# Opening and first turn of a fused attention kernel: GpSimd's and ScalarE's work reordered, q's first 128 pixels split apart, high blocks sent ahead of low ones

## The reference

```
q = Wq x + bq   (32 x 1024)      k = Wk x + bk   (32 x 1024)      v = Wv x + bv   (256 x 1024)
scores[i, j] = sum over channels of q[:, i] k[:, j]          (1024 x 1024)
attn = softmax(scores, over j)
out[:, i] = sum over j of v[:, j] attn[i, j]   + x[:, i]
```

## Time and profile before

| | us |
|---|---|
| median of three runs | 176.33 |
| the profiled execution's own time | 175.45 |
| its span | 173.3 |
| TensorE busy in it | 162.6 |
| VectorE busy | 137.0 |
| ScalarE busy | 110.6 |
| GpSimd busy | 41.1 |

### The profile page before, as it was taken

The page is one execution under the profiler, slowest core; times in us unless marked ns, Lnnn a source line. Parts: engine busy times, 40 slices in busy tenths (PEclk is TensorE's granted clock), DMA queues, the critical chain, the costliest instruction groups (busy, mean ns, idle before and its releaser), DMA issues.

```text
span 173.3 us, 2476 instructions
## 1 busy us (share of the span) xinstructions
PE 162.6 (94%) x814; PEld 129.9 (75%) x814; DVE 137.0 (79%) x215; ACT 110.6 (64%) x200; POOL 41.1 (24%) x50
## 2 busy tenths in 40 slices
PE   7979798978999999999999999999999999999992
PEld 5557676756888898767788898778888897776871
DVE  0779879888799898798899998799874889856353
ACT  2669594876985665777885665764884765665310
POOL 6249830042122030031222030042220020002500
PEclk9999999999999999999999999999999999999998
DMA  5941554034500320054400320054500330003003
GB/s 182 323 156 50 162 193 179 0 91 114 191 5 0 91 99 22 4 116 111 165 2 0 95 101 22 2 120 109 170 0 0 93 117 8 0 0 121 0 0 121
DMA packets 7500, 14.44 MB, mean 83 GB/s; under 512 B 1280, under 2 KB 1792, under 8 KB 7488
## 3 DMA queue, kind: packets, MB, share of 16 engines
q1 hardware_dynamic: 6656, 13.37, 24.0%
q0 software_dynamic: 416, 0.79, 2.1%
q10 hardware_dynamic: 416, 0.13, 0.3%
HBM read 4.59 MB, written 4.19 MB: 51 GB/s over the span
## 4 chain that ended last, share of the span: by engine, by line
PE 76%; DVE 12%; DMA 3%; ACT 3%; issue 2%; SPq 1%; DVEq 0%; ACTq 0%
PE acc L755 30%; PE acc L763 14%; PE slot L627 11%; PE st L741 8%; PE slot L680 7%; DVE negmax L514 5%; DMA wqk<-wqk_t 2%; DVE w_lo L557 1%; ACT dump L375 1%; SPq L195 1%; DMA k_a<-qk_parts 1%; PE slot L639 1%; PE st L726 1%; PE slot L644 1%; PE acc L759 1%
## 5 line engine op out<-in xcount | busy, mean ns | idle before, releaser
L755 PE MATMUL acc<-w_hi,v_hi 128*128 128x512 f32 x128 | 51.2, 400 | 0.0
L755 PE MATMUL acc<-w_hi,v_lo 128*128 128x512 f32 x128 | 50.5, 394 | 0.0
L406 ACT ACTIVATE w_full<-st 128x512 f32<-128x512 f32 x64 | 37.5, 594 | 17.1 <-PE st L741 17.1
L375 ACT ACTIVATE dump<-slot,negmax 128x1024 f32<-128x1024 f32 x29 | 32.4, 1117 | 13.5 <-DVE negmax L514 13.0
L314 POOL TENSOR_TENSOR w_lo<-w_full,w_hi 128x512 fp32r<-128x512 f32 x16 | 21.3, 1331 | 80.0 <-ACT w_full L406 64.0
L763 PE MATMUL acc<-w_lo,v_hi 128*128 128x512 f32 x120 | 38.4, 396 | 0.0
L514 DVE TENSOR_REDUCE negmax<-slot 128x1 f32<-128x1024 f32 x29 | 35.3, 1218 | 3.4 <-PE slot L680 3.4
L557 DVE TENSOR_TENSOR w_lo<-w_full,w_hi 128x512 fp32r<-128x512 f32 x48 | 33.2, 692 | 4.3 <-ACT w_full L406 0.6
L755 PEld LDWEIGHTS acc<-w_hi,v_hi 128*128 128x128 f32 x128 | 24.1, 189 | 5.6 <-issue 0.4
L548 DVE CAST w_hi<-w_full 128x512 fp32r<-128x512 f32 x47 | 19.9, 424 | 10.3 <-ACT w_full L406 9.1
L755 PEld LDWEIGHTS acc<-w_hi,v_lo 128*128 128x128 f32 x128 | 24.2, 189 | 5.2
(11 more groups left out here) (81 smaller groups left out, 178.5 us busy)
## 6 DMA issues: line engine op xcount, KB each, us to landing
out<-o_sb SPq DMA_DIRECT2D x7, 512.0 KB, 2.9
x_sb<-x SPq DMA_DIRECT2D x3, 1024.0 KB, 5.6
k_b<-k_a SPq DMA_DIRECT2D x8, 192.0 KB, 2.5
q_b<-q_a SPq DMA_DIRECT2D x8, 192.0 KB, 2.6
k_a<-qk_parts SPq DMA_DIRECT2D x12, 64.0 KB, 2.0
q_a<-qk_parts SPq DMA_DIRECT2D x12, 64.0 KB, 2.0
x_sb<-x SPq DMA_DIRECT2D x1, 512.0 KB, 3.6
x_sb<-x SPq DMA_DIRECT2D x2, 256.0 KB, 4.8
```

The source lines that it names most:

```text
L375: nc.scalar.activation(dump[:, t % 2, :], s_home(b, t), ACT.Exp, bias=negmax[:, t:t + 1], accum_out=rowsum[:, t:t + 1]).then_inc(rowsum_re ...
L406: nc.scalar.activation(w_full[:, r, :], st[:, j % 2, :], ACT.Exp).then_inc(exp_done, 1)
L755: nc.tensor.matmul(acc[:, c, :], v[:, j, ch], w_hi[:, r, :], start=(j == 0 and v is v_hi), stop=False)
```

## The change

- `cut_by_act` loses tile 7 of each turn: its `w_hi` is no longer a second exponential on ScalarE but a cast on VectorE.
- SP's `first_stacks` issues the high blocks of both halves, and then the low blocks of both, where it went half by half.
- `put_q_lo` takes a range of pixels, and runs for the first 128 pixels, the next 384, and the second half: three operations for two. The waits for `q_lo_put` are recounted, and `first_scores(1)` gets a wait for the second of them.
- `wv_hi` is made by GpSimd, which waits for the last `x_lo` of image 0 and for wv; it and `wv_lo` stand ahead of GpSimd's first `put_q_dup`, where `wv_lo` stood behind it.
- On ScalarE `sum_exp(0, TH)` goes from ahead of the first turn to behind its first exponential (tile 2), and `cut_x` in each step goes behind `put_rows`.

```diff
--- before.py
+++ after.py
@@ -32,7 +32,7 @@
 
 
     def cut_by_act(n):
-        return n % PER in ((0, 1, 7, 9, 11) if n < PER else (0, 7, 9, 11))
+        return n % PER in ((0, 1, 9, 11) if n < PER else (0, 9, 11))
 
 
     def split_by_pool(n):
@@ -230,6 +230,7 @@
                     sp.wait_ge(qk_cut_done, 2 * (b - 1) + h + 1)
                     blocks(sp, k_a, 0, 0, h, ka_in[h])
                     blocks(sp, q_a, 0, 1, h, qa_in[h])
+                for h in range(2):
                     sp.wait_ge(qk_split, 2 * (b - 1) + h + 1)
                     blocks(sp, k_a, 1, 2, h, ka_in[h])
                     blocks(sp, q_a, 2, 3, h, qa_in[h])
@@ -241,7 +242,7 @@
                 sp.wait_ge(k_lo_put, h + 1)
                 sp.wait_ge(k_hi_put, h + 1)
                 second_stack(k_b, k_a, h, kb_in[h])
-                sp.wait_ge(q_lo_put, h + 1)
+                sp.wait_ge(q_lo_put, h + 2)
                 sp.wait_ge(q_dup_put, h + 1)
                 second_stack(q_b, q_a, h, qb_in[h])
             for b in range(2, BATCH):
@@ -330,18 +331,22 @@
                     parts[:, :, :].bitcast(fp32).rearrange("p c (g d r) -> p c g d r", g=2, d=2)[:, :, :, 0, :],
                 ).then_inc(pair_made, 1)
             pool.wait_ge(pair_made, 2)
-            put_q_dup(0)
-            pool.wait_ge(q_dup_put, 1)
+
+            pool.wait_ge(x0_split, 4)
+            pool.wait_ge(wv_in, DMA)
+            nc.gpsimd.tensor_copy(wv_hi[:, :, :], wv[:, :, :]).then_inc(wv_cut, 1)
             pool.wait_ge(wv_cut, 1)
             nc.gpsimd.tensor_tensor(wv_lo[:, :, :], wv[:, :, :], wv_hi[:, :, :].bitcast(fp32),
                                     ALU.subtract).then_inc(wv_split, 1)
+            pool.wait_ge(wv_split, 1)
+            put_q_dup(0)
+            pool.wait_ge(q_dup_put, 1)
             prepare_x1(0)
             pool.wait_ge(x1_split, 1)
             put_q_dup(1)
             pool.wait_ge(q_dup_put, 2)
             for i in range(1, 3):
                 prepare_x1(i)
-
             pool.wait_ge(shift_ready, 1)
             prepare_x1(3)
             for n in range(TILES):
@@ -427,8 +432,6 @@
             put_k_hi(1)
             put_q_hi(0)
             put_q_hi(1)
-            act.wait_ge(wv_in, DMA)
-            nc.scalar.activation(wv_hi[:, :, :], wv[:, :, :], ACT.Copy).then_inc(wv_cut, 1)
             for t in range(TH):
                 sum_exp(0, t)
             log_sums(0, 0)
@@ -438,17 +441,18 @@
             exp(0)
             first_cut_v(3)
             exp(1)
-            sum_exp(0, TH)
 
             def turn(b):
                 for s in range(PER):
                     if PER * b + s + AHEAD < TILES:
                         exp(PER * b + s + AHEAD)
-                    if s in CUT_X and b + 2 < BATCH:
-                        cut_x(b + 2, CUT_X.index(s))
+                    if b == 0 and s == 0:
+                        sum_exp(0, TH)
                     what, k, image = front(b, s)
                     if what == ROW:
                         put_rows(b + image, k)
+                    if s in CUT_X and b + 2 < BATCH:
+                        cut_x(b + 2, CUT_X.index(s))
                     what, t, image = front(b, s - 1)
                     if what == S:
                         sum_exp(b + image, t)
@@ -490,12 +494,15 @@
                     out=k_a[2 * CQK:3 * CQK, cols(h)], in0=qk_home(0, h)[0:CQK, :], scalar=bias[0:CQK, 0:1],
                     in1=k_a[0:CQK, cols(h)].bitcast(fp32), op0=ALU.add, op1=ALU.subtract).then_inc(k_lo_put, 1)
 
-            def put_q_lo(h):
+            def put_q_lo(part):
+
+                h = part.start // HALF
                 rows = slice(2 * CQK, 3 * CQK)
                 dve.wait_ge(q_hi_put, h + 1)
                 nc.vector.scalar_tensor_tensor(
-                    out=q_a[CQK:2 * CQK, cols(h)], in0=qk_home(0, h)[rows, :], scalar=bias[rows, 0:1],
-                    in1=q_a[rows, cols(h)].bitcast(fp32), op0=ALU.add, op1=ALU.subtract).then_inc(q_lo_put, 1)
+                    out=q_a[CQK:2 * CQK, part], in0=qk_home(0, h)[rows, part.start - h * HALF:part.stop - h * HALF],
+                    scalar=bias[rows, 0:1], in1=q_a[rows, part].bitcast(fp32),
+                    op0=ALU.add, op1=ALU.subtract).then_inc(q_lo_put, 1)
 
             def split_qk(b, h):
                 dve.wait_ge(qk_cut_done, 2 * (b - 1) + h + 1)
@@ -570,10 +577,11 @@
             dve.wait_ge(bias_in, DMA)
             put_k_lo(0)
             put_k_lo(1)
-            put_q_lo(0)
+            put_q_lo(slice(0, P))
+            put_q_lo(slice(P, HALF))
             for t in range(TH):
                 row_max(0, t)
-            put_q_lo(1)
+            put_q_lo(cols(1))
             first_cut_v()
             shifts(0, 0)
             split_v(0, 0)
@@ -682,11 +690,13 @@
                 last.then_inc(scores_ready, 1)
 
             def first_scores(t):
-                if t == 3:
+                if t == 1:
+                    pe.wait_ge(q_lo_put, 2)
+                elif t == 3:
                     pe.wait_ge(rowsum_ready, 1)
                 elif t == TH:
                     pe.wait_ge(q_dup_put, 2)
-                    pe.wait_ge(q_lo_put, 2)
+                    pe.wait_ge(q_lo_put, 3)
                     pe.wait_ge(v_split, 1)
                 elif t == TH + 1:
                     pe.wait_ge(v_split, 4)
```

## The result

The changed kernel took 174.47 us in the median of 4 runs (173.03 to 174.81), the kernel before 176.28 (4 runs, 175.70 to 176.50). The ratio is 0.990, with a 95% interval of 0.987 to 0.993. The forecast was 173.8, in a range of 172.4 to 175.1: the time lies in the range, the gain is 1.8 us where 2.55 were forecast. The 47 executions of the kernel before that ran beside the experiments took 175.25 to 176.58, with a median of 175.86. Against those the gain is 1.4 us and not 1.8: the first four of the kernel before were on the slow side. The spread of the changed kernel, 2.3 us where the kernel before has 1.3, turns out to be the main thing that the forecast did not see.

The account below looks back on a forecast made before the run. TensorE, busy 162.6 of 173.3 us, was taken as the bound, so only its idle places could yield. Terms 1.9 + 0.4 - 0.1 + 0.35 = 2.55 from 175.45 gave 172.9, plus 0.88 for the median 173.8 us; range 172.4 to 175.1.

Parts of the forecast that it names:

- q_lo split: Opening: with the first 128 pixels of q_lo separate, q_dup decides the first scores, 0.22 us earlier.
- The lock-out: Opening: VectorE's shift subtraction no longer excluded by GpSimd's subtraction, 0.16 for 1.28 us, 1.12 gained, with 0.3 us of margin.
- sum_exp: First turn, tile 2: VectorE's cast no longer idles behind ScalarE's exponential sum of scores 4; 1.0 us gained.
- Tile 7 against SP's order: First turn, last k_a block: VectorE's added cast loses 0.5 us, SP's high blocks sent first gain 0.26.
- Tile 8 behind it: First turn: GpSimd's w_lo of tile 9 falls beside VectorE's work on tile 8; 0.2 us lost, bounds nothing and 0.5.
- Turn 1: Removing the wait before tile 8 gains 0.9 us, VectorE's late finish gives back 0.5; net 0.4.
- Turn 2: Wait before tile 8 worth 0.38 us, against the same 0.5 lost at VectorE's finish: -0.1.
- Turn 3: No projection behind it and VectorE not full, so 0.35 us of gain stays.
- the lock-out stays: Rival, opening: GpSimd 0.3 us or more later, shifts meet part 2's subtraction; 1.12 less gained, 174.9 us, chance 0.20.
- the opening is hidden: Rival: the k_a wait ends nearly where it did, only turns 1 to 3 count, 0.65; 175.7 us, chance 0.06.
- VectorE blocked in front of the finish: Rival: GpSimd's tile 9 precedes VectorE's tile 8, each finish waits up to 1.3 us; 178.3 us, chance 0.07.
- The third sign: Sign of a wrong forecast: turns 1 and 2 are longer than before.

Follow-up runs that it names:

- e6: The kernel before with only part 2 of GpSimd's x1 preparation moved behind the wait for the shifts: 175.04 us, ratio 0.994.
- e12: The changed kernel with tile 7's w_hi on ScalarE in every turn and the first q_lo whole again: 172.81 us.
- e7: The changed kernel with wv_hi on ScalarE and wv_lo behind GpSimd's first q_dup again: 174.79 us.
- e2: The changed kernel with sum_exp(0, TH) ahead of the first turn again: 175.58 us.
- e4: The changed kernel with SP's blocks half by half, high then low, again: 173.82 us.
- e1: The changed kernel with tile 7's w_hi back on ScalarE in every turn: 172.00 us, ratio to the kernel before 0.978.
- e3: The changed kernel with cut_x ahead of put_rows again: 173.42 us.
- e5: The changed kernel run again without any edit, 8 executions: 174.50 us.
- e10: The changed kernel with tile 7's w_hi on ScalarE in turns 0 to 2 and on VectorE in turn 3 only: 173.30 us.
- e11: As e10, and SP also waits for x0's last piece before it issues the load of x1: 172.55 us.

## Why the prediction was right, and where its sum was not

*q_lo split, 0.22.* Right in place, q_dup now decides. x_lo to first scores went from 3.08 to 2.90, 0.18; but with a late x0 it is 2.94 without the split too (e6, e12), so the split is worth 0.04 there. Over-sized.

*The lock-out, 1.12.* Right in place and size: 0.16 us in place of 1.28, e6 1.08, e7 1.13. The 0.3 us of margin held: GpSimd's part 2 ended at 18.77, the subtraction came at 19.13.

*sum_exp, 1.0.* Right: e2 1.09.

*Tile 7 against SP's order, -0.5 and +0.26.* The step "SP is free: 0.26 gained" failed as a term of its own: the new cast spreads VectorE's two operations 2.68 us apart, longer than SP's four issues, so the old order is as good (e4). The cast itself costs 0.35 (e1), not 0.5. Of the 2.18 us gained to S1 the three terms above take 0.18 + 1.12 + 1.09; what is left, -0.21, is near the forecast sum of -0.24. That the two errors cancel is luck.

So 2.18 us to S1, where 2.1 were forecast. The wait behind it was forecast as about 2 us and seen as a row in the timeline, no more: *that TensorE's clock might fall in it is the term that the prediction left out.* It costs 1.4 us in half of the executions.

*Tile 8 behind it, -0.2.* The lock-out of tiles 8 and 9 came as described, -0.32: the next scores start 2.49 after S1 (44.20), before 2.17. In e3, where VectorE is first, it is 2.18.

*Turn 1, +0.9 and -0.5.* The wait removed gave its 0.89 (from the row matmuls to the first matmul behind tile 8's scores, 2.82 before and 1.93 after). Of that 0.36 went before S2: 0.09 for w_lo of tile 7, and 0.26, for which the profile names no releaser, most likely for k_a's last block: issued at 77.95, it was 2.3 us on its way, where the last one of the first turn took 1.9. TensorE, coming later by that, found the finish less late, -0.21. Net 0.32, forecast 0.4. The size is right; a wait there was not in the forecast.

*Turn 2, +0.38 and -0.5.* Up to S3 0.38 was gained and 0.49 lost, all around tile 7: 0.16 at its late w_hi and 0.32 at its late w_lo; then 0.47 was lost on the finish. *The step "against the same 0.5: -0.1" failed:* it priced the cast at the finish alone, and TensorE waits for the cast's own tile first. -0.58 measured for -0.1, the largest miss of the sum.

*Turn 3, 0.35.* 0.38: from the row matmuls to the first matmul behind tile 8's scores 2.30 before and 1.92 after. Right.

2.18 - 0.32 + 0.32 - 0.58 + 0.38 = 1.98, against 2.08 by the table. 1.4 us of lower clock in half of the executions take 0.7 of it, which leaves 1.4 us, as the 47 executions beside the experiments have it. The 1.8 of the first comparison has some 0.4 of chance in it, four executions of each kernel. So the forecast of 2.55 was too high by 0.5 us of terms (turn 2 above all) and 0.7 of clock, and that 174.47 lies inside the range owes something to its width. The rivals "the lock-out stays" and "the opening is hidden" did not come; "VectorE blocked in front of the finish" came in small, by the order forecast, in the first turn.

The forecast also named its own signs of being wrong. The shift subtraction takes 0.16 us, as it should. k_a's wait ended at 41.71, later than the 41.5 named, but x_lo ended 1.18 later than in the profile of before; at equal landing it is 8.16 + 32.37 = 40.53, against the 40.6 forecast (first scores 11.06 against 11.0, row matmuls 18.57 against 18.5). The third sign did come: turn 2 is longer than before (S2 to S3 38.77 against 38.45), which is the failed step above.

## What to carry to other kernels

An edit that frees one engine by loading another must be priced at every place where the other is the last to arrive: here the version without the one moved cast, e1, is the best of all, 172.0 us and 2.2% under the kernel before (172.8 in e12, whose profile is as long from x_lo's end on; x0 landed later there), while with the cast 1 us of that and the clock were given back. Gains ahead of a fixed wait lengthen that wait, so look at what a longer idle stretch does to TensorE's clock. Where VectorE's smallest instructions stand on the path, look for GpSimd instructions beside them. Where a load at the start lands at varying times, compare distances from its end, and sort the executions by their mean clock before comparing medians.

## What the runs showed of the hardware that was not expected

TensorE's granted clock fell to half for about 3 us (0.62 and 0.53 in two stretches of 2 us, e5) after 1.71 us without matmuls, and the mean clock shows such a fall in 21 of the 46 executions of kernels with a wait of 1.64 to 1.72 us in their profile. The other 25 executions of the same kernels do not have it, nor do the 83 of kernels with a wait of 1.34 us or less. A one-input cast of 128x4 on VectorE was held 1.1 us by a GpSimd subtraction (e7). Of two subtractions of 128x512, the one that started later took 1.57 us on VectorE (changed kernel, 0.69 alone) or 1.73 on GpSimd (e3, 1.3 alone). The landing of the last 256 KB of x0 varied so that x_lo ended between 8.16 and 9.39 in kernels that request x1 at once, and was at 7.97 and 7.99 in the two that wait with it. The span ended 1 us later than usual behind the last VectorE operation, which the final 256 KB transfers follow, in the two kernels e10 and e11.
